# Key products of the first batch of null and masked attention inside the normalisation; null weights loaded during the routed experts

## The chip, the cores and the metric

One core of a Trainium2 chip runs the whole kernel. The metric is device time in microseconds (us); the median of three runs before the change is 2725.27 us (2724.52 to 2727.11).

## The reference

Eight residual layers on x of shape (8 batches, 256 positions, 256 features), all float32. Each adds a function of the normalised x to x. In order: a depooling layer, attention with registers, attention over a context, routed experts, null attention, a feed-forward layer with signs as weights, masked attention, and a last block with attention over positions and experts.

```python
x = x + _L1_ffn_ref(_layernorm(x, axis=-1), L1_ffn_router_w, L1_ffn_w1, L1_ffn_w2)
x = x + _L2_xattn_ref(_layernorm(x, axis=-1), ctx_2048, L2_xattn_Wq, L2_xattn_Wkv, L2_xattn_null_kv, ...)
x = x + _L2_ffn_ref(_layernorm(x, axis=-1), L2_ffn_k0, L2_ffn_k1, L2_ffn_k2, ...)
x = x + _L3_xattn_ref(ctx_2048, _layernorm(x, axis=-1), mask_BxS2_fk1, mask_BxS2_fk1, L3_xattn_W_src, ...)
```

Null attention has 16 heads of 64: queries from the normalised x, keys and values from the context (8, 256, 512), and one learned key and value more. Masked attention has 8 heads of 32; its keys, too, come from the context alone. So the keys of both need nothing of the layer's own normalisation.

## The kernel before

Activations are stored feature by position: `X` and `XN` are [128 partitions, 2, 2048 positions]. A layer is a row of blocks; at the end of a block all engines meet at a barrier. Inside a block each engine has a queue of its own, written out in order, and waits on semaphores of the others.

**Normalisation** (`layer_norm_phase`, L187). The 2048 positions are four groups (0 to 3) of 512. TensorE (L227 to L267) first makes the mean sums of all four groups, each in its own PSUM bank (4 to 7), then spreads means 0 and 1 over the partitions; then, per group: `variances` (sum of squares), `spread_mean` two groups ahead, `spread_inverse`. `chunk_sums` (L232) and `spread` (L238) are the helpers under whose lines its matmuls stand. ScalarE (ACT) loads its table for the square root if it isn't there (L288), copies the mean sums (L291), squares (L275) and takes roots (L279). VectorE (DVE) centres (L309), inverts (L316) and scales (L330). SyncE (SP) issues the layer's loads here (`prefetch`), and GpSimd (POOL) does `prepare`; the phase ends when all are through.

**Attention stream** (`attention_stream`, L554). One block after the normalisation. Before the first scores come the uses in `first`: in null attention a product of null values with output weights (L790), then the twelve products `front` of batch 0: query (L1649) and key (L1660) products in turn, four of each, and four value products (L1672). In masked attention: query (L1918), key (L1931) and value (L1945) product. Each goes into a PSUM bank (0 to 3 in turn) and is taken from there by VectorE or ScalarE. From then on the products of the next batch are interleaved with scores, exponentials and values by a fixed plan. The context of each batch is loaded in this block by SyncE, two batches ahead at most.

**Loads.** Null attention's weights are loaded in its normalisation (L1625 to L1631). Masked attention's are loaded in its own normalisation, first the mask row (L1895), which GpSimd turns into `drop` and `mrows` (L1906, L1907), then the weights (L1898).

**Routed experts** (L1374): four groups of eight experts; SyncE waits in that block for the experts' weights and has nothing else to do.

Of the kernel before, what the change touches and what calls it, by code (L numbers as in the profile page):

```python
# [82 lines left out]
def build(nc, A, out):  # L83
    top = ExitStack()
    with top:
# [43 lines left out]
        if STAGES >= 3:  # L129
            context_attention_layer(g)  # L130
            end_layer()
        if STAGES >= 4:
            routed_ffn_layer(g)
            end_layer()
        if STAGES >= 5:
            null_attention_layer(g)
            end_layer()
# [49 lines left out]
def layer_norm_phase(g, tag, src=None, dst=None, gain=None, shift=None, resid=None, rms_gain=None, eps=None,  # L187
                     prefetch=None, prepare=None, by_position=False, loaded=None, aside=None):
# [16 lines left out]
    def part(t, gi):  # L205
        return t[:, :, gi * GT:(gi + 1) * GT]

    with nc.Block() as block:
# [19 lines left out]
        def _(pe):  # L228
            def chunk_sums(bank, c0, of):
                for k in range(KD):  # L230
                    for c in range(4):
                        mm = pe.matmul(bank[32 * c:32 * c + 32, c0:c0 + P], mean[:, 0:32], of[:, k, c * P:(c + 1) * P],  # L232
                                       start=(k == 0), stop=(k == KD - 1))
                return mm
# [35 lines left out]
        def _(act):  # L270
# [6 lines left out]
            def root(gi):  # L277
                act.wait_ge(var_ready, gi + 1)
                act.activation(g.ln_std[:, gi % 2], g.bank[4 + gi][:, P:2 * P], ACT.Sqrt, bias=eps[:]).then_inc(rooted, 1)  # L279
# [9 lines left out]
            for gi in range(NG):  # L289
                act.wait_ge(mean_ready, gi + 1)  # L290
                act.activation(g.ln_mean[:, gi], g.bank[4 + gi][:, 0:P], ACT.Copy).then_inc(mean_copied, 1)  # L291
# [14 lines left out]
        def _(v):  # L306
# [32 lines left out]
            for gi in range(NG):  # L339
# [3 lines left out]
                scale(gi)  # L343
            v.wait_ge(scaled, NG)
# [209 lines left out]
def attention_stream(g, ctx, tag, heads, dh, groups, keys, front, front_at, q_of, k_of, v_of, slot_of, project, finish,  # L554
                     wl, n_weights, mask=None, own_keys=False, load=None, n_loads=0, load_after=None, null=None, reg=None):
# [35 lines left out]
    ld = [g.sem(f"{tag}_loaded{j}") for j in range(2)] if n_loads else None  # L591
# [36 lines left out]
    first += [("front", 0, k) for k in range(len(front))]  # L628
    slots = []
# [37 lines left out]
    def shared_bank(use):  # L667
        n = ready_at[use] - 1
        return g.bank[n % 4] if n < len(first) else M

    with nc.Block() as block:
        @block.sync
        def _(sp):
            if n_loads:
                for b in range(B):
# [24 lines left out]
        def _(pe):  # L700
# [60 lines left out]
            def shared(use):  # L761
                bank = shared_bank(use)
                before = ready_at[use] - 1 - (4 if ready_at[use] <= len(first) else 1)
                if before >= (0 if ready_at[use] <= len(first) else len(first)):
# [55 lines left out]
            for use in first:  # L820
# [30 lines left out]
        def _(act):  # L851
# [38 lines left out]
            for use in first:  # L890
# [33 lines left out]
        def _(v):  # L924
# [78 lines left out]
            for use in first:  # L1003
# [370 lines left out]
def routed_ffn_layer(g):  # L1374
# [18 lines left out]
    with ExitStack() as ctx:  # L1393
# [208 lines left out]
def null_attention_layer(g):  # L1602
    nc, A = g.nc, g.A
# [3 lines left out]
    with ExitStack() as outer:  # L1607
        gain = g.sb("na_gain", [P, KD], F32, outer)
        shift = g.sb("na_shift", [P, KD], F32, outer)
        with ExitStack() as ctx:  # L1610
            sb = lambda n, s, dt=F32: g.sb("na_" + n, s, dt, ctx)
            Wq = sb("Wq", [P, KD, INNER])
            Wkv = sb("Wkv", [P, KC, 2 * INNER])
            Wo = sb("Wo", [P, IC, D])
            cxT = sb("cxT", [P, 2, KC, N])
# [3 lines left out]
            nv = sb("nv", [P, IC, H])  # L1619
            nk = sb("nk", [P, IC])  # L1620
            wl, nkl, placed = g.sem("na_weights"), g.sem("na_null_loaded"), g.sem("na_null_placed")

            def prefetch(sp):
                for half in range(2):
                    sp.dma_start(nk[half * DH:(half + 1) * DH, :], A["L2_null_key"]).then_inc(nkl, 16)  # L1625
                sp.dma_start(Wq[:], feature_rows(A["L2_xattn_Wq"])).then_inc(wl, 16)
                sp.dma_start(Wkv[:], feature_rows(A["L2_xattn_Wkv"])).then_inc(wl, 16)
                sp.dma_start(Wo[:], feature_rows(A["L2_xattn_Wout"])).then_inc(wl, 16)
                sp.dma_start(nv[:].rearrange("p k h -> p (k h)"), A["L2_null_values"]).then_inc(wl, 16)
                sp.dma_start(gain[:], A["L2_xattn_ln_scale_col"]).then_inc(wl, 16)  # L1630
                sp.dma_start(shift[:], A["L2_xattn_ln_bias_col"]).then_inc(wl, 16)  # L1631
# [7 lines left out]
            layer_norm_phase(g, "n2x", prefetch=prefetch, prepare=prepare)  # L1639
# [5 lines left out]
            for m0 in range(0, IC, 2):  # L1645
# [11 lines left out]
                def k_product(pe, bank, b, m0=m0):  # L1657
                    for m in range(2):
# [25 lines left out]
            def finish(v, bank, b):  # L1684
# [9 lines left out]
                             null={"values": nv, "out": Wo})  # L1694
# [176 lines left out]
def masked_attention_layer(g):  # L1871
    nc, A = g.nc, g.A
    H, DH = 8, 32
    with ExitStack() as ctx:
# [16 lines left out]
        wl, ml, st = g.sem("ma_weights"), g.sem("mk_loaded"), g.sem("mk_step")  # L1891

        def prefetch(sp):
# [3 lines left out]
            for t, name in ((Ws, "L3_xattn_W_src"), (Wt, "L3_xattn_W_tgt"), (Wo, "L3_xattn_W_out")):  # L1897
# [4 lines left out]
            sp.dma_start(bv[:], A["L3_xattn_b_src"][D:2 * D].unsqueeze(0)).then_inc(wl, 16)  # L1902
# [7 lines left out]
        layer_norm_phase(g, "n3x", prefetch=prefetch, prepare=prepare)  # L1910
# [512 lines left out]
```

## Time and profile before

| | us |
|---|---|
| median of 3 runs | 2725.27 |
| the profiled execution | 2728.62 |
| its span in the trace | 2726.7 |
| TensorE busy | 2361.6 (87%) |
| VectorE busy | 1294.5 (47%) |
| ScalarE busy | 995.9 (37%) |
| GpSimd busy | 128.2 (5%) |

The span is the time from the first to the last instruction in the profile. Times in the rows are counted from its start. A float32 product of the program stands in the trace as two matmuls. PEclk is TensorE's granted clock, where 1.00 is 2.4 GHz and 0.50 is 1.2 GHz.

### The profile page before, as it was taken

Reading aid. Unit: us, or ns where it says so; the run is one execution under the profiler, and the core shown is the slowest. Engines: PE = TensorE matmul, PEld = TensorE weight load, DVE = VectorE, ACT = ScalarE, POOL = GpSimd, SP = SyncE. Lnnn points to the kernel's source line nnn. Section 1 sums busy time; section 2 is a strip of 40 time slices with the busy share of each in tenths; the row PEclk is TensorE's granted clock in tenths of the full one; section 3 lists DMA queues with packets and bytes.
Section 4 is the critical chain, followed back from the end, with each engine's and each line's share of the span. In section 5 each row is a group of like instructions: output and inputs, shape, how many; then the busy total and the mean of one; then the engine's idle time right before and its main releaser. Section 6 shows DMA issues by size and latency. Waiting matters only on the chain. (4 is left out here: it accounts for less than half of the span.)

```text
span 2726.7 us, 38491 instructions
## 1 busy us (share of the span) xinstructions
PE 2361.6 (87%) x15045; PEld 1680.3 (62%) x15045; DVE 1294.5 (47%) x2609; ACT 995.9 (37%) x2834; POOL 128.2 (5%) x206
## 2 busy tenths in 40 slices
PE   6778887999988999989999999969988897874984
PEld 4455555666655666666666666547876675654773
DVE  6456665777764334333455445654443443231003
ACT  3245564777762111112333333433223442231122
POOL 0000000000000000000000000030010000002003
PEclk8979999999998999999999999999999999796996
DMA  3000001000002000020000000000011000021332
GB/s 113 16 1 1 1 1 40 13 25 13 24 1 93 1 0 1 1 109 8 9 9 9 8 9 1 1 28 0 1 43 40 20 5 16 1 72 61 124 113 66
DMA packets 52534, 74.81 MB, mean 27 GB/s; under 512 B 8050, under 2 KB 41348, under 8 KB 51204
## 3 DMA queue, kind: packets, MB, share of 16 engines
q1 hardware_dynamic: 50820, 68.14, 7.4%
q0 software_dynamic: 1536, 4.20, 0.5%
q8 instruction: 123, 2.02, 0.3%
q14 instruction: 55, 0.45, 0.1%
HBM read 63.94 MB, written 8.39 MB: 27 GB/s over the span
## 5 line engine op out<-in xcount | busy, mean ns | idle before, releaser
L862 ACT ACTIVATE ca_prob<-bank,ca_nmax 128x512 f32<-128x512 f32 x256 | 174.0, 690 | 92.9 <-DVE ca_nmax L929 92.9
L929 DVE TENSOR_REDUCE ca_nmax<-bank 128x1 f32<-128x512 f32 x256 | 164.0, 682 | 56.2 <-PE bank L720 56.1
L862 ACT ACTIVATE na_prob<-bank,na_nmax 128x257 f32<-128x257 f32 x256 | 118.0, 474 | 191.0 <-DVE na_nmax L929 191.0
L1458 PE MATMUL bank<-XN,rf_W 128*128 128x512 f32 x384 | 172.9, 601 | 0.0
L1469 PE MATMUL bank<-rf_W,rf_h 128*128 128x256 f32 x768 | 170.8, 379 | 0.0
L1469 PEld LDWEIGHTS bank<-rf_W,rf_h 128*128 128x128 f32 x768 | 145.9, 190 | 33.1 <-issue 14.8
L734 PEld LDWEIGHTS bank<-cst,ca_prob 128*128 128x128 f32 x1024 | 112.3, 142 | 73.6 <-issue 63.2
L862 ACT ACTIVATE ra_prob<-bank,ra_nmax 128x256 f32<-128x256 f32 x256 | 118.2, 482 | 104.1 <-DVE ra_nmax L929 104.1
L1513 ACT ACTIVATE rf_r<-bank 128x512 f32<-128x512 f32 x96 | 57.4, 598 | 256.3 <-PE bank L1458 256.3
L734 PE MATMUL bank<-cst,ca_prob 128*128 128x128 f32 x1024 | 140.5, 279 | 6.6 <-DVE ca_pT L935 5.9
L929 DVE TENSOR_REDUCE na_nmax<-bank 128x1 f32<-128x257 f32 x256 | 90.8, 417 | 91.5 <-PE bank L720 91.5
L1660 PE MATMUL bank<-na_cxT,na_Wkv 128*128 128x256 f32 x512 | 117.8, 383 | 5.5 <-DVE na_q L1654 5.5
L1458 PEld LDWEIGHTS bank<-XN,rf_W 128*128 128x128 f32 x384 | 73.2, 193 | 79.8 <-issue 78.7
L1566 DVE TENSOR_TENSOR rf_h<-rf_r 128x512 f32<-128x512 f32 x96 | 66.1, 692 | 113.9 <-ACT rf_r L1513 113.9
L1778 PE MATMUL bank<-sf_h,sf_W 128*128 128x512 f32 x512 | 120.1, 395 | 0.0
L1672 PE MATMUL bank<-na_Wkv,na_cxT 128*128 128x512 f32 x256 | 115.4, 595 | 0.0
L1660 PEld LDWEIGHTS bank<-na_cxT,na_Wkv 128*128 128x128 f32 x512 | 95.0, 190 | 25.9 <-DVE na_q L1654 11.8
L1778 PEld LDWEIGHTS bank<-sf_h,sf_W 128*128 128x128 f32 x512 | 95.9, 187 | 23.5
L720 PE MATMUL bank<-ca_k,ca_qz 32*128 32x512 f32 x512 | 73.7, 642 | 26.0 <-ACT ca_prob L862 25.1
L935 DVE COPY ca_pT<-bank 128x512 f32<-128x512 f32 x128 | 87.4, 683 | 17.4 <-PE bank L734 17.2
L238 PE MATMUL bank<-ln_rstd,cst 128*128 128x128 f32 x352 | 51.8, 291 | 49.8 <-DVE ln_rstd L316 49.8
L929 DVE TENSOR_REDUCE ra_nmax<-bank 128x2 f32<-128x512 f32 x128 | 82.0, 681 | 22.4 <-PE bank L720 22.4
(395 smaller groups left out, 4423.8 us busy)
## 6 DMA issues: line engine op xcount, KB each, us to landing
xl_w<-in_L_ffn_w SPq DMA_DIRECT2D x16, 1024.0 KB
dp_cx<-in_ctx_tok SPq DMA_DIRECT2D x4, 1024.0 KB, 14.1
ca_v<-in_ctx_values SPq DMA_DIRECT2D x8, 512.0 KB, 4.6
rf_W<-in_L_ffn_w SPq DMA_DIRECT2D x8, 512.0 KB, 8.6
na_Wkv<-in_L_xattn_Wkv SPq DMA_DIRECT2D x1, 4096.0 KB
na_cxT<-in_ctx SPq DMA_DIRECT2D x8, 512.0 KB, 3.4
ma_cxT<-in_ctx SPq DMA_DIRECT2D x8, 512.0 KB, 3.3
X<-in_x SPq DMA_DIRECT2D x1, 2048.0 KB, 7.9
```

The lines of the kernel that those rows point to most:

```text
L720: mm = pe.matmul(S[u][:, hh * keys:(hh + 1) * keys], q_of(hs[hh], i, b), k_of(hs[hh], i, b), start=(mask is None), stop=(hh == per - 1), s ...
L734: mm = pe.transpose(TB[f % 2][:, j * P:(j + 1) * P], prob[:, n % 2, u, c0:c0 + P], ident)
L862: e = act.activation(prob[:, n % 2, u, hh * keys:(hh + 1) * keys], S[u][:, hh * keys:(hh + 1) * keys], ACT.Exp, bias=nmax[:, n % 2, u, hh: ...
L929: v.tensor_reduce(nmax[:, n % 2, u], S[u][:, 0:W].rearrange("p (h k) -> p h k", h=per), AX.X, ALU.max, negate=True).then_inc(maxed, 1)
L935: v.tensor_copy(o, TB[f % 2][:].rearrange("p (j q) -> p j q", j=4)).then_inc(copied_v, 1)
L1458: mm = pe.matmul(g.bank[n % 3][:], W1[:, k, c * P:(c + 1) * P], g.XN[:, k, gi * GT:(gi + 1) * GT], start=(k == 0), stop=(k == KD - 1))
L1469: mm = pe.matmul(output(i, t), h[:, n % 8, t * P:(t + 1) * P], W2[:, n % CH], start=(n == own[0]), stop=(n == own[-1]), skip_group_check=True)
L1513: act.activation(r[:, n % 3], g.bank[n % 3][:], ACT.Relu).then_inc(relu, 1)
L1566: v.tensor_tensor(h[:, n % 8], r[:, n % 3], r[:, n % 3], ALU.mult).then_inc(squared, 1)
L1660: mm = pe.matmul(bank[:, m * N:(m + 1) * N], Wkv[:, k, (m0 + m) * P:(m0 + m + 1) * P], cxT[:, b % 2, k], start=(k == 0), stop=(k == KC - 1))
L1672: mm = pe.matmul(bank[:], cxT[:, b % 2, k, t * P:(t + 1) * P], Wkv[:, k, INNER + half * 512:INNER + (half + 1) * 512], start=(k == 0), sto ...
L1778: mm = pe.matmul(g.bank[m % 4][:], W1[:, k, m * P:(m + 1) * P], h[:, k, s], start=(k == 0 and s == 0), stop=(k == C1 - 1 and s == 1))
```

## The change

The normalisation gets `fill`, an object with halves of key products to issue between its own matmuls and with copies to make behind its own copies. To free banks 6 and 7 for them, mean sums and variances of four groups share banks 4 and 5. Null attention issues key products `front[1]` and `front[3]` of batch 0 at places 0 to 3; place 0 is before `variances(0)`, place n behind `variances(n - 1)`. Masked attention issues its one key product at places 2 and 3. The stream leaves these out of `first`. Null's weights and the context of its batch 0 are allocated before the routed experts and loaded by SyncE in that block. Masked attention loads the context of batch 0 with its weights, in a new order.

```diff
 def layer_norm_phase(...)
+    def mean_at(gi):
+        return slice(gi // 2 * P, (gi // 2 + 1) * P)
+    def var_at(gi):
+        return slice(2 * P + gi // 2 * P, 2 * P + (gi // 2 + 1) * P)
...
             def variances(gi):
                 pe.wait_ge(squared, gi + 1)
-                chunk_sums(g.bank[4 + gi], P, g.ln_sq[:, gi % 2]).then_inc(var_ready, 1)
+                if gi >= 2:
+                    pe.wait_ge(rooted, gi - 1)
+                chunk_sums(g.bank[4 + gi % 2], var_at(gi), g.ln_sq[:, gi % 2]).then_inc(var_ready, 1)
...
             for gi in range(NG):
-                chunk_sums(g.bank[4 + gi], 0, part(src, gi)).then_inc(mean_ready, 1)
+                if gi >= 2:
+                    pe.wait_ge(mean_copied, gi - 1)
+                chunk_sums(g.bank[4 + gi % 2], mean_at(gi), part(src, gi)).then_inc(mean_ready, 1)
             spread_mean(0)
             spread_mean(1)
+            if fill is not None:
+                fill.multiply(pe, 0)
             for gi in range(NG):
                 variances(gi)
+                if fill is not None:
+                    fill.multiply(pe, gi + 1)
                 if gi + 2 < NG:
                     spread_mean(gi + 2)
                 spread_inverse(gi)
...
                 root(gi)
+                if fill is not None:
+                    fill.take(act, "a", gi + 1)
...
                 scale(gi)
+                if fill is not None:
+                    fill.take(v, "v", gi + 1)
 def attention_stream(...)
+    early_uses = [("front", 0, k) for k, _ in early]
+    first = early_uses + [use for use in first if use not in early_uses]
...
+        if n < len(early):
+            return g.bank[6 + n % 2]
+        return g.bank[(n - len(early)) % 4] if n < len(first) else M
...
+        def multiply(pe, place):
+            for n, (k, places) in enumerate(early):
+                for half in range(2):
+                    if places[half] == place:
+                        if half == 0:
+                            pe.wait_ge(wl, 16 * n_weights)
+                            if n_loads:
+                                pe.wait_ge(ld[0], 16 * n_loads)
+                            if n >= 2:
+                                wait_freed(pe, early_uses[n - 2])
+                        mm = front[k][1](pe, shared_bank(early_uses[n]), 0, half)
+                        if half == 1:
+                            mm.then_inc(ready, 1)
+        def take(engine, who, place):
+            for n, (k, places) in enumerate(early):
+                if places[1] == place and freer(early_uses[n]) == who:
+                    engine.wait_ge(ready, n + 1)
+                    front[k][2](engine, shared_bank(early_uses[n]), 0).then_inc(freed_v if who == "v" else freed_a, 1)
+    if norm is not None:
+        norm(Early)
...
-                for b in range(B):
+                for b in range(0 if norm is None else 1, B):
...
 def routed_ffn_layer(g, next_weights):
...
                 for e in range(E):
                     sp.wait_ge(weights[e], 32)
+                next_weights.load(sp)
...
+    def load(self, sp):     # class NullWeights
+        for half in range(2):
+            sp.dma_start(self.nk[half * self.DH:(half + 1) * self.DH, :], A["L2_null_key"]).then_inc(self.null_loaded, 16)
+        sp.dma_start(self.Wkv[:], feature_rows(A["L2_xattn_Wkv"])).then_inc(self.loaded, 16)
+        sp.dma_start(self.cxT[:, 0], feature_rows(A["ctx"][:, 0:N])).then_inc(self.context_loaded[0], 16)
+        sp.dma_start(self.Wq[:], feature_rows(A["L2_xattn_Wq"])).then_inc(self.loaded, 16)
...
 null attention:
+                             null={"values": nv, "out": Wo}, norm=norm, early=[(1, (0, 1)), (3, (2, 3))],
+                             ld=w.context_loaded)
 masked attention:
         def prefetch(sp):
+            sp.dma_start(Ws[:], feature_rows(A["L3_xattn_W_src"])).then_inc(wl, 16)
+            sp.dma_start(bv[:], A["L3_xattn_b_src"][D:2 * D].unsqueeze(0)).then_inc(wl, 16)
+            sp.dma_start(cxT[:, 0], feature_rows(A["ctx"][:, 0:N])).then_inc(context_loaded[0], 16)
             m1 = A["mask_BxS2_fk1"].rearrange("b n -> (b n)")
             sp.dma_start(mrow[:], m1.unsqueeze(0).to_broadcast([P, T])).then_inc(ml, 16)
...
         def k_take(v, bank, b):
+            if b == 0:
+                v.wait_ge(ml, 32)
...
+                         norm=norm, early=[(1, (2, 3))], ld=context_loaded)
```

## Rows read from the trace of the kernel before

**Rows 1.** The page: busy time by engine, and a kind of DMA issue.
```profile
PE 2361.6 (87%) x15045; PEld 1680.3 (62%) x15045; DVE 1294.5 (47%) x2609; ACT 995.9 (37%) x2834; POOL 128.2 (5%) x206
...
ma_cxT<-in_ctx SPq DMA_DIRECT2D x8, 512.0 KB, 3.3
```

**Rows 2.** Timeline, null's normalisation: start us, length us, instruction, [idle before and releaser].
```profile
1202.06 0.64 PE L232 MATMUL bank<-ln_sq,cst 128*32 128x128 f32 x16 [1.51 <-ACT ln_sq L275]
...
1202.64 1.16 PE L238 MATMUL bank<-ln_mean,cst 128*128 128x128 f32 x8
...
1204.30 1.16 DVE L309 TENSOR_TENSOR ln_cent<-X,bank 128x1024 f32<-128x1024 f32 x1
...
1205.64 1.22 DVE L330 TENSOR_TENSOR XN<-ln_cent,bank 128x1024 f32<-128x1024 f32 x1 [0.17 <-PE bank L238]
...
1209.05 1.22 DVE L330 TENSOR_TENSOR XN<-ln_cent,bank 128x1024 f32<-128x1024 f32 x1 [0.17 <-PE bank L238]
...
1211.26 1.16 PE L238 MATMUL bank<-ln_rstd,cst 128*128 128x128 f32 x8 [1.68 <-DVE ln_rstd L316]
...
1215.79 1.22 DVE L330 TENSOR_TENSOR XN<-ln_cent,bank 128x1024 f32<-128x1024 f32 x1 [1.25 <-PE bank L238]
```

**Rows 3.** Timeline, head of null's attention stream.
```profile
1217.55 3.61 PE L790 MATMUL bank<-na_Wo,na_nv 128*16 128x256 f32 x16 [1.80 <-PEq L208]
...
1222.93 3.62 PE L1660 MATMUL bank<-na_cxT,na_Wkv 128*128 128x256 f32 x16
...
1226.38 1.89 PE L1649 MATMUL bank<-XN,na_Wq 128*128 128x256 f32 x8
1226.64 0.60 ACT L1665 ACTIVATE na_k<-bank 128x512 f32<-128x512 f32 x1 [13.21 <-PE bank L1660]
```

**Rows 4.** Timeline, masked normalisation and head of its stream.
```profile
2031.32 7.11 POOL L1906 TENSOR_SCALAR ma_drop<-ma_mrow 128x2048 bf16<-128x2048 f32 x1 [185.18 <-DMA ma_mcol<-in_mask_col]
...
2035.08 0.65 PE L232 MATMUL bank<-ln_sq,cst 128*32 128x128 f32 x16
...
2038.50 5.38 POOL L1907 TENSOR_SCALAR ma_mrows<-ma_mrow 128x2048 f32<-128x2048 f32 x1
...
2045.35 1.22 DVE L330 TENSOR_TENSOR XN<-ln_cent,bank 128x1024 f32<-128x1024 f32 x1 [1.25 <-PE bank L238]
...
2047.09 1.97 PE L1918 MATMUL bank<-XN,ma_Wt 128*128 128x256 f32 x8 [1.78 <-PEq L208]
...
2052.29 5.15 PE L1931 MATMUL bank<-ma_cxT,ma_Ws 128*128 128x256 f32 x16 [3.24 <-DMA ma_cxT<-in_ctx]
...
2057.37 0.69 PE L1943 MATMUL bank<-ma_bv,cst 1*128 1x256 f32 x2
2057.48 0.88 DVE L1937 SCALAR_TENSOR_TENSOR ma_k<-bank,ma_bs,ma_mrow 128x256 f32<-128x256 f32 x2 [7.44 <-PE bank L1931]
...
2063.57 0.40 PE L716 MATMUL bank<-ma_drop,onesb 1*128 1x512 bf16 x4 [1.04 <-issue]
```

**Rows 5.** Windows, masked: stretch, length, busy time by engine, PEclk, DMA share, GB/s.
```profile
2033.00:2034.00 1.00, 0.36 (x5) 0.17 (x3) 1.00 (x2) 0.00 (x0) 1.00 (x1) 1.00 1.06 385
...
2036.00:2037.00 1.00, 0.81 (x8) 0.62 (x6) 1.00 (x2) 0.36 (x2) 1.00 (x1) 1.00 0.07 18
...
2052.00:2053.00 1.00, 0.71 (x2) 0.62 (x3) 0.00 (x0) 0.00 (x0) 0.00 (x0) 0.50 0.07 25
```

**Rows 6.** Timeline, mean sums and first copies in three other normalisations.
```profile
438.78 1.95 PE L232 MATMUL bank<-X,cst 128*32 128x128 f32 x64 [2.56 <-PEq L102]
...
440.15 0.92 ACT L291 ACTIVATE ln_mean<-bank 128x128 f32<-128x128 f32 x4
...
822.40 3.11 PE L232 MATMUL bank<-X,cst 128*32 128x128 f32 x64 [2.01 <-PEq L102]
...
2262.34 2.65 PE L232 MATMUL bank<-X,cst 128*32 128x128 f32 x64 [2.00 <-PEq L102]
```

**Rows 7.** Windows, first routed expert products behind the normalisation at 822.
```profile
846.00:850.00 4.00, 4.00 (x14) 3.16 (x15) 0.00 (x0) 0.39 (x2) 0.00 (x0) 0.50 0.00 0
```

More of the change, by code:

```diff
@@ L554, in attention_stream @@
 def attention_stream(g, ctx, tag, heads, dh, groups, keys, front, front_at, q_of, k_of, v_of, slot_of, project, finish,
-                     wl, n_weights, mask=None, own_keys=False, load=None, n_loads=0, load_after=None, null=None, reg=None):
+                     wl, n_weights, mask=None, own_keys=False, load=None, n_loads=0, load_after=None, null=None, reg=None,
+                     norm=None, early=(), ld=None):
     nc = g.nc
@@ L590, in attention_stream @@
                                       "widened", "scaled"))
-    ld = [g.sem(f"{tag}_loaded{j}") for j in range(2)] if n_loads else None
+    if ld is None and n_loads:
+        ld = [g.sem(f"{tag}_loaded{j}") for j in range(2)]
     S = [g.bank[u] for u in range(4)]
@@ L763, in shared @@
                 before = ready_at[use] - 1 - (4 if ready_at[use] <= len(first) else 1)
-                if before >= (0 if ready_at[use] <= len(first) else len(first)):
+                if before >= (len(early) if ready_at[use] <= len(first) else len(first)):
                     wait_freed(pe, order[before])
@@ L818, in shared @@
                 mm.then_inc(ready, 1)
-            for use in first:
+            for use in first[len(early):]:
                 shared(use)
@@ L888, in shared @@
                 e.then_inc(freed_a, 1)
-            for use in first:
+            for use in first[len(early):]:
                 shared(use)
@@ L1001, in shared @@
                     v.wait_ge(reg_inverted, use[1] + 1)
-            for use in first:
+            for use in first[len(early):]:
                 shared(use)
@@ L1606, in null_attention_layer, with __init__ @@
     IC = INNER // P
[L1607 to L1610, printed above, removed]
+    def __init__(self, g, outer, ctx):
+        sb = lambda n, s: g.sb("na_" + n, s, F32, ctx)
+        self.g = g
+        self.gain = g.sb("na_gain", [P, KD], F32, outer)
+        self.shift = g.sb("na_shift", [P, KD], F32, outer)
+        self.Wq = sb("Wq", [P, KD, self.INNER])
+        self.Wkv = sb("Wkv", [P, KC, 2 * self.INNER])
+        self.Wo = sb("Wo", [P, self.IC, D])
+        self.nv = sb("nv", [P, self.IC, self.H])
+        self.nk = sb("nk", [P, self.IC])
+        self.cxT = sb("cxT", [P, 2, KC, N])
+        self.loaded, self.null_loaded = (g.nc.alloc_semaphore(name="na_" + n) for n in ("weights", "null_loaded"))
+        self.context_loaded = [g.nc.alloc_semaphore(name=f"na_loaded{j}") for j in range(2)]
@@ L1611, in null_attention_layer @@
+def null_attention_layer(g, w, outer, ctx):
+    nc, A = g.nc, g.A
+    H, DH, INNER, IC = w.H, w.DH, w.INNER, w.IC
+    gain, shift, Wq, Wkv, Wo, nv, nk, cxT, wl, nkl = (w.gain, w.shift, w.Wq, w.Wkv, w.Wo, w.nv, w.nk, w.cxT, w.loaded,
+                                                      w.null_loaded)
+    with outer:
+        with ctx:
             sb = lambda n, s, dt=F32: g.sb("na_" + n, s, dt, ctx)
[L1612 to L1613 removed]
@@ L1618, in null_attention_layer @@
             vv = sb("v", [P, 2, 2, INNER])
[L1619 to L1631, printed above, removed]
+            placed = g.sem("na_null_placed")
             def prepare(po):
@@ L1655, in q_take, with k_product @@
                                              None, ALU.mult)
-                def k_product(pe, bank, b, m0=m0):
-                    for m in range(2):
+                def k_product(pe, bank, b, half=None, m0=m0):
+                    for m in range(2) if half is None else (half,):
                         for k in range(KC):
@@ L1926, in q_take, with k_product @@
             return o
-        def k_product(pe, bank, b):
-            for m in range(KD):
+        def k_product(pe, bank, b, half=None):
+            for m in range(KD) if half is None else (half,):
                 for k in range(KC):
```

48 lines of the change are left out of this document (29 added, 19 removed).

## The prediction, made before the changed kernel was run

> **What bounds the kernel now.** I read the page's first two parts, then the timelines of the two stretches that the change rewrites, then the start of every other normalisation, and last the granted clock. TensorE is busy in 87% of the span and DVE in 47% [rows 1], so work taken off TensorE in a stretch that it bounds is time. The chain of waits on the page covers only the last 25 us, so each stretch is judged from its timeline.
>
> Each normalisation runs four groups in turn (0 to 3): TensorE sums squares, TensorE spreads the next mean and the inverse root, DVE inverts, centres, scales. In null's the scalings of groups 0 and 1 start 3.41 us apart (1205.64, 1209.05), and DVE fills that with a reciprocal, a centring of 1.16 and a scaling of 1.22. TensorE is not full: it stands idle 1.51 us before the first sum of squares and 1.68 us before the third spread of the inverse [rows 2]. After the barrier the picture turns round: from 1217.55 TensorE runs without a gap, with the null product (3.6 us), then query and key products in turn; the first key product begins at 1222.93 and the query product behind it at 1226.38, 3.45 us later, as in the pairs that follow [rows 3]. That stretch is bound by TensorE.
>
> Masked attention starts otherwise. TensorE does the query product at 2047.09, waits 3.24 us for batch 0's context, and does the key product in 5.15 us, not 3.6, since in the pause its clock went from 2.4 to 1.2 GHz (granted 0.50 in the slice from 2052) [rows 4, 5]. The value product follows at 2057.37 and the first scores at 2063.57.
>
> **Null attention, the stream.** Two key products leave the head of the stream: 2 x 3.45 = **6.9 us** less of unbroken TensorE work. The takers are no limit there: ACT needs 0.60 us for a key product, below the 1.73 us of the shortest product, and waits 13.21 us for its first [rows 3]. I take the full 6.9. Bounds: 0 (something else ends the head last, such as DVE's copies of the values) to 7.2 (two rows of 3.62).
>
> **Null attention, the normalisation.** The four halves cost 1.72 us each. Before sum 0 the pause is 1.51, so the first half costs 0.2. The second stands between the sum of squares 0 and the spread of mean 2, which DVE wants: that spread moves from 1202.64 to 1204.58, centring 2 from 1204.30 to 1205.76, and the scaling of group 0 from 1205.64 to 1206.93 (+1.3) [rows 2]. The third does the same to mean 3: sum of squares 1 at 1206.64, the half to 1208.94, the spread of mean 3, centring at 1210.13, scaling 1 at 1211.30 where it was 1209.05 (+2.25). The fourth falls into the pause of 1.68 us and costs nothing more by itself; square, root and reciprocal of group 2, now queued behind the late centring, bring the scalings 2 and 3 to +2.4. ACT's two copies of 0.60 stand in its idle time. The normalisation ends **2.4 us** later. Bounds: 1.3 (only the first displaced spread counts) to 5.2 (three halves outside the pause).
>
> The loads themselves move from SP's queue in the normalisation to that in the routed experts, behind that stage's own weights, which are down by its first items; nine DMAs run beside some 340 us of expert products. Before, nobody waited on them either: TensorE started 0.54 us after the last scaling of null's normalisation, and 0.52 after the masked one [rows 2, 3, 4]. So 0. Null's scalings beside such traffic (1205.64) and after it (1215.79) both take 1.22 us [rows 2]; a stretch of the last digit in them, 1%, over the 20 us that the loads last would be 0.2 us, the bound on either side. SP's own waits there are met some 300 us before the barrier.
>
> **Masked attention, the stream.** The key product and the wait for the context both go: the scores stood 16.48 us behind the start of the query product [rows 4]. Without them: query product 1.9, then from the first value product to the scores 6.2 (2057.37 to 2063.57), sum 8.1. Gain **8.4 us**, if the clock stays up, which it did until the pause. Bounds: 3.2 (the wait alone) to 8.4.
>
> **Masked attention, the normalisation.** Here the weights are not loaded ahead: the first half waits, behind sum of squares 1, for all seven loads. Before, the DMA engines were done with them at about 2036.3: 385 GB/s in the slice from 2033, 18 in that from 2036 [rows 5]. The context adds 512 KB ahead of them [rows 1]; at 385 GB/s that is 1.4 us, so about 2037.7. TensorE reaches the half at 2035.08 + 0.58 = 2035.66: a new wait of **2.0 us** (bounds 0 to 3). Behind it in TensorE's queue are the spread of mean 3 and of the inverse 1, which DVE waits for. With the half's 1.72 that spread starts at 2039.4 for 2035.66; DVE's own work had covered 0.6 of that, as in null's rounds (scaling 0 there waits 0.17, the centring ahead of it stands 0.5 behind its spread), so scaling 1 comes 3.1 later, 2.0 of it the wait. The second half falls in the pause. Then DVE takes the key product itself, two operations in 0.88 us [rows 4], between scaling 2 and reciprocal 3, on the chain that ends the phase: +0.9, and the rest of the shift through ACT's late root makes **4.2 us** in all. Bounds: 2.1 (no wait) to 5.2 (3 us of wait).
>
> GpSimd: the mask row now queues behind the context and a weight of twice its size, 1.57 MB; it came at 2031.32, and at 385 GB/s comes 4.1 us later, at 2035.4. Its 7.11 + 5.38 us [rows 4] end at 2047.9. The phase ends at 2046.57 + 4.2 = 2050.8 by DVE, so GpSimd has 2.9 us to spare. Were DVE not late it would end the phase at 2047.9, 1.3 us later than before; so that is the floor of this term if the wait is shorter.
>
> **All normalisations: two banks in place of four.** The mean sums of groups 2 and 3 now wait for ACT's copies of groups 0 and 1. ACT must first load its table and touch it: its first copy ends 1.63 us after TensorE's start (440.15 + 0.26 - 438.78) [rows 6]. TensorE at 2.4 GHz would begin sum 2 after 0.98 (64 matmuls in 1.95): a new pause of 0.70 us with the 0.05 of a signal, and everything of that phase comes later by it. This holds for context's normalisation and for the two at 1790.9 and 2437.9 which show the same 1.95 and 0.92: 3 x 0.70 = 2.1. At 2262.34 the sums take 2.65 and the clock falls among them; sum 2 would start at 2263.3, and now at 2264.0: 0.7. At 822.40, where they take 3.11, sum 2 would start at 823.8 and now at 824.1: 0.3. In the other six the sums run at 1.2 GHz from the start or no table is loaded, and the copy is there in time. Sum **3.2 us**; bounds 0 (the copies' timing hides it) to 11 x 0.7 = 7.7. The waits on the variance side are met long before.
>
> **The sum.** -6.9 + 2.4 - 8.4 + 4.2 + 3.2 = **-5.5 us**. The profiled execution took 2728.62 us, 1.9 beyond its span and 3.3 above the median of the runs; nothing in these terms scales with that, so they are taken off the median: 2725.27 - 5.5 = **2719.8 us**.
>
> **Rivals.** (A) is the sum above, with its likeliest terms: 2717.5 to 2722.
> (B) The fillings cost less: the mean sums don't pause, or the weights are there. Without the masked wait the phase ends at 2048.7 by DVE, 2.1 late and not 4.2: 2717.7. Without the 3.2 as well: 2714.5. For it: in the last slice of the loads only 18 GB/s moved, small transfers whose order is not seen. Against: TensorE has to wait for a count that includes the last of them.
> (C) The clock. After null's and the masked normalisation TensorE's clock was up (the query product's 8 matmuls of 256 columns in 1.97 us [rows 4]), but after the one at 822 it was at 0.50 for four us and more of expert products [rows 7]. The same phase with the same work ended in both ways. One such fall more (masked, where the normalisation gets a 2 us wait and a longer thin tail) costs half of its length. The row shows four us of it; I take ten, since the slices on either side of the row are slow in part, and so 5 us: 2724.8. The present one going away gives 2715.
> The Trainium skill ("TensorE: Matmul & The Clock Gate", Part 1) says that the throttled state is the default and activity releases it, and that the monitor runs free of the kernel's start. Rows 4 and 5 agree with the first half: idle from 2049, at 0.50 by 2052 [rows 4, 5]. By this rule a stall inside a thin phase is what makes (C); it also lets the filled null phase hold its clock better, and does not say which; it changes no term of the sum.
> (D) Slower: the new pauses behind the mean sums, each on top of the 2 to 3 us of idle at the barrier ahead, drop the clock in the four normalisations that have them and in the masked one. Priced as in (C), 5 us each; it decides from the third such fall: +15 - 5.5 gives 2734.8. Two leave 2729.8, still within 0.2%. Against it: 0.7 us is small beside the 1.5 us pauses that these phases have already with the clock up.
> That the products are not early at all is excluded: the order of the queues is written out.
>
> **How the numbers follow.** A measurement of this kernel can tell about 0.2%, 5.45 us, from no change; the forecast of -5.5 stands on that bound. (A) 0.42, half on either side; (B) 0.25, faster; (C) 0.20, within; (D) 0.08, slower; 0.05 for a better clock or an unseen cost. Faster 0.49, within 0.2% 0.42, slower 0.09. The range holds (A), (B) and most of (C), with room for one clock episode on either side: 2712 to 2728.
>
> **What would show it.** In null: key products at four places of the normalisation, its last scaling 2.4 us later against the phase's first sum, the stream's first scores 6.9 us earlier against its null product. In masked: a TensorE wait ahead of the first half that a DMA of the weights ends, 2 us; scaling 3 4.2 us later against the phase's start; no wait for the context, value products right behind the query product at clock 1.00; GpSimd done before DVE. In context's normalisation a TensorE idle of 0.7 us released by ACT's copy. Wrong it would be by a TensorE clock of 0.50 in a stretch where it is 1.00 now, by GpSimd ending the masked phase, or by a stream head that did not shorten by the product's time.

## The result and the profile after

The changed kernel takes 2736.91 us (median of 22 runs, 2724.11 to 2747.91), the kernel before 2726.07 (22 runs beside it, 2714.58 to 2732.61). The ratio is 1.0038, 95% interval 1.0024 to 1.0053: it is slower, where the prediction said 2719.8 and gave "slower" 0.09. Single runs of the changed kernel fall into two groups, eleven up to 2735.2 and eleven from 2738.6 on; the profiled execution, 2731.23 us, is of the first.

The page after shows nothing of it at first sight: TensorE is busy for 3.6 us more, and the line of its clock reads almost alike.

```profile
span 2729.4 us, 38507 instructions
PE 2365.2 (87%) x15045; PEld 1679.9 (62%) x15045; DVE 1294.9 (47%) x2609; ACT 996.1 (36%) x2834; POOL 128.3 (5%) x206
```

A table of stages tells more. A stage is taken here from ACT's first use of its square root (L288, L307 after) in one normalisation to that in the next. The stretch ahead of the first row (87.4 us before and after) and the one behind the last (33.2 before, 32.5 after) are left out. In y3 that use stands behind the copies, so its borders lie up to 4 us later. Times are us.

```
stage             before  again(z3)  after  x0     y1     y2     y3     x3     y4     z1
registers          352.7   349.7     354.8  354.9  355.0  349.7  351.4  352.6  351.2  351.5
context            383.6   387.5     389.6  389.6  388.5  385.5  385.1  383.6  383.7  385.5
routed experts     372.6   368.4     373.2  373.3  370.8  372.4  370.1  372.4  372.4  368.2
null               596.0   598.3     592.8  592.8  596.1  594.4  592.7  595.9  594.3  594.3
null, second norm.  23.9    23.9      26.0   26.0   26.2   23.7   25.2   23.7   23.7   23.7
signs              210.1   210.0     210.9  210.9  210.9  210.7  209.0  210.2  210.8  210.5
masked             237.4   237.4     240.0  240.1  234.4  240.5  245.0  233.9  235.3  236.3
positions          175.6   175.6     163.2  163.2  178.8  174.0  179.4  162.5  168.9  173.9
experts            254.4   254.7     259.1  255.0  255.7  254.3  252.9  255.2  254.2  254.5
```

(The labels are those of the experiments below.) Against the first trace of the kernel before, the changed kernel wins 3.2 us in null and loses 2.1 with registers, 6.0 in context, 2.1 and 0.8 around null's second normalisation and 2.6 in masked. Two traces of the kernel before differ by 3 to 4 us in registers, context and routed experts, so one pair of columns says little there. All fourteen traces together say more. The five with two banks and the early table (after, x0, y1, x1, x2) have registers at 354.5 to 355.0, context at 388.5 to 389.6 and null's second normalisation at 26.0 to 26.2; the nine others have 349.7 to 352.7, 383.6 to 387.5 and 23.7 to 25.3. In the profiled execution positions gives 12.4 back, in attention code that the change doesn't touch (of that stage it touches the normalisation). Had it stood at 175.6 there as well, this execution would have taken 2743.6, which is where the second group of runs lies; that is inferred, no execution of that group was profiled. TensorE's clock goes with the stage's time: over the whole of it the mean is 0.89 in the kernel before and 0.98 after. A window in it shows the same; the stage begins 11 us later after than before, so the three windows don't hold quite the same work.

Windows of 2360 to 2400, before, after and x1; columns as in [rows 5].

```profile
2360.00:2400.00 40.00, 34.61 (x185) 25.10 (x184) 11.29 (x29) 9.68 (x39) 1.23 (x2) 0.84 0.00 1
```

```profile
2360.00:2400.00 40.00, 33.64 (x207) 25.05 (x208) 13.09 (x33) 13.50 (x56) 1.23 (x2) 1.00 0.00 1
```

```profile
2360.00:2400.00 40.00, 34.92 (x174) 24.89 (x172) 9.99 (x26) 10.03 (x40) 0.61 (x1) 0.79 0.00 0
```

**Null.** The timeline after answers to [rows 2, 3]. The half at 1211.61 pushes the spread of mean 2 to 1213.44; the last scaling ends 2.4 us later against the phase's first sum, as forecast. Then the null product, 3.61 us before, takes 4.90: the clock has fallen at the end of the phase. The first scores come 33.4 us behind that product's start and not 39.1: a gain of 5.6, not 6.9. In all eight traces with null's early products this product takes 4.9 to 6.6 us; of the six without them, five have 3.61.

```profile
1213.44 1.05 PE L249 MATMUL bank<-ln_mean,cst 128*128 128x128 f32 x8
...
1226.95 1.22 DVE L351 TENSOR_TENSOR XN<-ln_cent,bank 128x1024 f32<-128x1024 f32 x1 [1.25 <-PE bank L249]
...
1228.72 4.90 PE L847 MATMUL bank<-na_Wo,na_nv 128*16 128x256 f32 x16 [1.80 <-PEq L219]
```

**Masked.** The timeline answers to [rows 4]. The first half waits 3.29 us for the last of seven loads and then runs at 1.2 GHz (3.42 us; the second half, at 2.4 GHz, 1.99). The phase takes 27.5 us from its first sum, 7.1 more than before. The context wait is gone, but query and value products run at 1.2 GHz again, and the scores come 12.15 us behind the query product where I had 8.1. GpSimd, started by the mask at 2045.12, is done at 2057.7, ahead of DVE.

```profile
2034.63 2.11 PE L243 MATMUL bank<-X,cst 128*32 128x128 f32 x64 [2.57 <-PEq L102]
...
2045.12 7.11 POOL L1988 TENSOR_SCALAR ma_drop<-ma_mrow 128x2048 bf16<-128x2048 f32 x1 [190.69 <-DMA ma_mcol<-in_mask_col]
...
2047.63 3.42 PE L2014 MATMUL bank<-ma_cxT,ma_Ws 128*128 128x256 f32 x8 [3.29 <-DMA ma_bo<-in_L_xattn_b_out_col]
...
2060.90 1.22 DVE L351 TENSOR_TENSOR XN<-ln_cent,bank 128x1024 f32<-128x1024 f32 x1 [1.25 <-PE bank L249]
...
2062.64 3.75 PE L2001 MATMUL bank<-XN,ma_Wt 128*128 128x256 f32 x8 [1.78 <-PEq L219]
...
2074.79 0.40 PE L773 MATMUL bank<-ma_drop,onesb 1*128 1x512 bf16 x4 [1.03 <-issue]
```

**Context**, where no product was moved, loses most against the first trace before. The timeline answers to [rows 6]: the two first mean sums take 1.08 us, then TensorE is idle for 0.60 us until ACT has copied the first, as forecast. But the other two and the spreads then run at 1.2 GHz (1.71 and 3.02 us, the spreads 2.05 before), and once more the first 16 matmuls of the next block: 6.64 us, 3.69 before.

```profile
440.91 1.08 PE L243 MATMUL bank<-X,cst 128*32 128x128 f32 x32 [2.56 <-PEq L102]
...
442.58 1.71 PE L243 MATMUL bank<-X,cst 128*32 128x128 f32 x32 [0.60 <-ACT ln_mean L310]
444.23 3.02 PE L249 MATMUL bank<-ln_mean,cst 128*128 128x128 f32 x16
...
464.20 6.64 PE L1343 MATMUL bank<-XN,ca_Wqkv 128*128 128x256 f32 x16 [1.81 <-PEq L219]
```

Windows of the same two places:

```profile
442.00:446.00 4.00, 3.42 (x40) 3.02 (x41) 0.00 (x0) 1.24 (x6) 0.71 (x1) 0.61 0.83 260
...
464.00:468.00 4.00, 3.80 (x9) 3.11 (x10) 0.00 (x0) 0.00 (x0) 0.00 (x0) 0.50 0.64 180
```

### The profile page after: what moved, and what is told of

Its sections match the earlier page's. It is cut to its first block and busy times, and to the rows that moved or that the text cites. A ratio compares the mean times of both kernels' runs of the same rounds, so it can differ in the third digit from the quotient of the medians.

```text
span 2729.4 us, 38507 instructions
## 1 busy us (share of the span) xinstructions
PE 2365.2 (87%) x15045; PEld 1679.9 (62%) x15045; DVE 1294.9 (47%) x2609; ACT 996.1 (36%) x2834; POOL 128.3 (5%) x206
## 3 DMA queue, kind: packets, MB, share of 16 engines
q8 instruction: 123, 2.02, 0.3%
## 5 line engine op out<-in xcount | busy, mean ns | idle before, releaser
L992 DVE COPY ca_pT<-bank 128x512 f32<-128x512 f32 x128 | 87.4, 683 | 17.2 <-PE bank L791 17.2
L1637 DVE SCALAR_TENSOR_TENSOR rf_acc<-bank,rf_comb,rf_acc 128x256 f32<-128x256 f32 x112 | 49.0, 479 | 90.9 <-PE bank L1527 90.9
## 6 DMA issues: line engine op xcount, KB each, us to landing
na_Wkv<-in_L_xattn_Wkv SPq DMA_DIRECT2D x1, 4096.0 KB, 13.2
```

Of the source, the lines that this page charges most:

```text
L992: v.tensor_copy(o, TB[f % 2][:].rearrange("p (j q) -> p j q", j=4)).then_inc(copied_v, 1)
```

## The experiments

Three sets (x, y, z) of four kernels; those of a set share a chip and the runs of the kernel before (medians 2724.29, 2725.25, 2725.44). Each had 10 to 12 runs.

### x0_after_again: the changed kernel once more

> The changed kernel once more, as a yardstick for the three beside it and for a second trace. All theories: about 10 us slower than before. If its single runs fall again into two clusters (about 2727 and 2742), then the trace with the lower mean granted clock (0.948 to 0.950 against 0.954) shows in which stage the second cluster loses its time.

Measured: 2727.16 us (2720.05 to 2745.82), ratio 1.0028 (1.0004 to 1.0051). Nine runs to 2733, three from 2742 on. The trace is of the first group and repeats the one above stage by stage but for experts (column x0); so no trace shows the second group. The kernel is slower again, though its interval begins just above 1 and its median lies 9.8 us below the first; its losses in registers and context are no accident of one execution.

### x1_masked_undone

```diff
-        def norm(early):
-            layer_norm_phase(g, "n3x", prefetch=prefetch, prepare=prepare, fill=early)
+        layer_norm_phase(g, "n3x", prefetch=prefetch, prepare=prepare)
...
-                         norm=norm, early=[(1, (2, 3))], ld=context_loaded)
+                         )
```

The masked layer's loads, their order and the place of its first context go back too.

> The changed kernel with the masked layer as it was (no early key product, context loaded in the stream, old order of loads). Theory M (the masked half's wait for all seven loads, 3.3 us in the trace and not 2.0, plus the clock that falls in that wait and again at the end of the phase): 3 to 8 us faster than the changed kernel, so +3 to +7 us against before. Theory B (the waits of the mean sums in all eleven normalisations): no difference to the changed kernel, +10.

Measured: 2730.87 (2724.09 to 2735.85), ratio 1.0023 (1.0008 to 1.0038). Against x0 the median is 3.7 higher and the mean 0.4 higher (2730.8, 2730.4): no difference. Its masked stage is 6 us shorter than x0's (234.1), but positions stands at 176.3 where x0 had 163.2. Theory M is not needed for the loss and alone does not undo it. The undone layer shows something else. Its key product waits 1.37 us for the context here, not 3.24, keeps its clock, and the scores stand 13.18 us behind the query product, not 16.48:

```profile
2057.61 3.72 PE L2010 MATMUL bank<-ma_cxT,ma_Ws 128*128 128x256 f32 x16 [1.37 <-DMA ma_cxT<-in_ctx]
```

Of the eight traces with the masked layer undone or never changed, five are like this (x1, x2, x3, y1, y4: waits of 1.27 to 1.43) and three like [rows 4] (before, z3, z4: 3.18 to 3.24). Which one comes is not explained by any run.

### x2_loads_and_banks

Both early products undone, as above for masked, and for null:

```diff
-                layer_norm_phase(g, "n2x", prepare=prepare, fill=early)
+                layer_norm_phase(g, "n2x", prepare=prepare)
...
-                             null={"values": nv, "out": Wo}, norm=norm, early=[(1, (0, 1)), (3, (2, 3))],
+                             null={"values": nv, "out": Wo}, norm=norm,
```

> No early product anywhere: what is left of the change is two banks in place of four for the sums of all normalisations, and null's weights and first context loaded during the routed experts. Theory B: +3 by the pauses alone, up to +10 with clock falls behind them. Theory M: +3 and no more. Rival L (loads during the routed experts cost): as here, and in the next kernel too.

Measured: 2735.55 (2729.36 to 2745.01), ratio 1.0046 (1.0030 to 1.0062). With nothing left but banks and loads it is as slow as the whole change. Theory B or rival L.

### x3_loads_only

As x2, with four banks (`g.bank[4 + gi]`, columns 0 and 128) and without the two waits.

> Only null's weights and first context loaded during the routed experts; four banks, no early product, the masked layer as before. Theories M and B: no difference to before (within 2 us). Rival L: slower, +3 or more.

Measured: 2717.43 (2710.07 to 2723.83), ratio 0.9972 (0.9959 to 0.9986): faster than before, which neither theory had. Rival L falls. Between x2 and x3 lie only the banks and their waits: 18.1 us by the medians, more than the whole change costs; of the difference between their traces, 13.6 us stand in positions. The trace says where x3 gains against before, not why: positions 162.5 and masked 233.9; null and routed experts stand as before.

### y1_two_banks_pure

The kernel before, with

```diff
             for gi in range(NG):
-                chunk_sums(g.bank[4 + gi], 0, part(src, gi)).then_inc(mean_ready, 1)
+                if gi >= 2:
+                    pe.wait_ge(mean_copied, gi - 1)
+                chunk_sums(g.bank[4 + gi % 2], mean_at(gi), part(src, gi)).then_inc(mean_ready, 1)
```

and the same for the variances.

> The kernel before with one edit: sums of four groups in two banks, with the two waits for ACT's copies. Theory B (the pause of 0.6 to 0.7 us behind the second mean sum starts falls of TensorE's clock in context's, null-end's and expert normalisations): +8 to +14 us against before, with context's stage 5 to 6 us longer. Rival (the loads in the routed experts and the two banks cost only together): within 3 us of before.

Measured: 2733.57 (2726.85 to 2743.99), ratio 1.0036 (1.0021 to 1.0052), the size of the whole change. Theory B holds, with context 4.9 longer than in the first trace before, though only 1.0 longer than in z3. Its timeline in context has the pause of 0.60, slow sums behind it, and the slow head of the next block:

```profile
440.55 1.08 PE L238 MATMUL bank<-X,cst 128*32 128x128 f32 x32 [2.56 <-PEq L102]
442.23 1.83 PE L238 MATMUL bank<-X,cst 128*32 128x128 f32 x32 [0.60 <-ACT ln_mean L301]
...
463.90 6.55 PE L1296 MATMUL bank<-XN,ca_Wqkv 128*128 128x256 f32 x16 [1.80 <-PEq L214]
```

The cleanest place is null's second normalisation. In all nine traces without the pause its 64 sums run through at 2.4 GHz (1.95 to 2.11 us); in all five with it the second 32 fall to 1.2 (1.93 to 1.94 where the first took 1.08). Before, and y1:

```profile
1790.92 1.95 PE L232 MATMUL bank<-XN,cst 128*32 128x128 f32 x64 [1.05 <-PEq L671]
```

```profile
1797.65 1.93 PE L238 MATMUL bank<-XN,cst 128*32 128x128 f32 x32 [0.60 <-ACT ln_mean L301]
```

### y2_four_banks_elsewhere

```diff
+    shared = fill is not None
...
-                if gi >= 2:
+                if shared and gi >= 2:
                     pe.wait_ge(mean_copied, gi - 1)
```

with bank and columns by `shared` too.

> The changed kernel, but the nine normalisations that get no early product keep four banks and no wait. Theory B: 8 to 12 us faster than the changed kernel, so -3 to +2 against before. Theory M (masked is the cost): no more than 3 us faster than the changed kernel.

Measured: 2728.34 (2720.82 to 2729.32), ratio 1.0012 (0.9999 to 1.0024): 8.6 us below the median first measured for the changed kernel, though not below x0's, and with +3.1 by the medians just outside the -3 to +2 expected. Registers and context stand at 349.7 and 385.5. The masked stage keeps its loss (240.5). Its first half waited 2.02 us this time:

```profile
2036.52 3.63 PE L2015 MATMUL bank<-ma_cxT,ma_Ws 128*128 128x256 f32 x8 [2.02 <-DMA ma_bo<-in_L_xattn_b_out_col]
```

### y3_table_later

The changed kernel, two banks everywhere, with ACT's table load moved:

```diff
-            act.activation(g.hold[:], eps[:], ACT.Sqrt).then_inc(table_set, 1)
             for gi in range(NG):
                 act.wait_ge(mean_ready, gi + 1)
                 act.activation(g.ln_mean[:, gi], ...).then_inc(mean_copied, 1)
+            act.activation(g.hold[:], eps[:], ACT.Sqrt).then_inc(table_set, 1)
             square(0)
```

> The changed kernel with two banks everywhere, but ACT loads its square root table behind its four copies of the mean sums and not ahead of them, so that the copies are in time and the pause goes. Theory B in the form that the pause is the cause: as good as four banks, 8 to 12 us faster than the changed kernel. Rival (two groups in one bank are slow for another reason, such as the matmul writes and the copies meeting in a bank): no gain.

Measured: 2723.50 (2715.69 to 2736.50), ratio 0.9996 (0.9979 to 1.0013): 13.4 below the changed kernel's first median, 3.7 below x0's. Its interval lies clear of the changed kernel's first (1.0024 to 1.0053) and overlaps x0's a little. It is no slower than y2, which has four banks elsewhere: two groups in a bank do no harm, the pause does. No TensorE wait for the copies is left in its trace. That execution is one of its slower ones (2730.15): masked stands at 245.0, where the clock fell in the wait for the loads (3.33) and stayed down longer than in the other traces, and positions at 179.4. In context the 64 sums run through and the block behind starts at 2.4 GHz:

```profile
436.64 2.11 PE L243 MATMUL bank<-X,cst 128*32 128x128 f32 x64 [2.56 <-PEq L102]
...
457.74 3.69 PE L1343 MATMUL bank<-XN,ca_Wqkv 128*128 128x256 f32 x16 [1.80 <-PEq L219]
```

### y4_null_only_four

As y2, with the masked layer undone as in x1.

> The part of the change that should pay by theories M and B together: null's early products and its loads ahead, four banks in the other ten normalisations, the masked layer as before. Loads only measured about -7, null's part was -3 by the traces: -7 to -11 us against before. If null's early products cost by the clock: worse than loads only, above -7.

Measured: 2718.60 (2715.89 to 2727.09), ratio 0.9984 (0.9970 to 0.9998), by the medians -6.7, by the ratio -4, where -7 to -11 was expected; 9.7 below y2, which differs by the masked part only. So in company of four banks theory M holds. Against x3 null's early products gave nothing: its null stage is 1.6 shorter, the whole not. In this trace the clock falls behind the filled phase, and the null product takes 6.55 us for 3.61:

```profile
1217.52 6.55 PE L848 MATMUL bank<-na_Wo,na_nv 128*16 128x256 f32 x16 [1.80 <-PEq L220]
```

### z1_masked_needs_only

```diff
-            sp.dma_start(Ws[:], feature_rows(A["L3_xattn_W_src"])).then_inc(wl, 16)
+            sp.dma_start(Ws[:], feature_rows(A["L3_xattn_W_src"])).then_inc(keys_loaded, 16)
+            sp.dma_start(bs[:], A["L3_xattn_b_src_col"]).then_inc(keys_loaded, 16)
...
-                            pe.wait_ge(wl, 16 * n_weights)
+                            pe.wait_ge(early_wl or wl, 16 * (early_n or n_weights))
```

> Four banks in the nine normalisations without early products (as in y2), and the masked half waits only for what it reads: the source weights, their bias and the context, issued first. Theory M: its wait of 3.3 us and the clock fall in it go, GpSimd (mask row behind 1.5 MB) becomes the end of the phase; masked stage 234 to 236 us where y2 had 240.5, and 3 to 6 us faster than y2. Rival (the masked stage loses by the place of the product, not by the wait): as y2, 2728.

Measured: 2720.12 (2714.93 to 2721.63), ratio 0.9979 (0.9969 to 0.9989), 8.2 below y2, of another set. The wait is gone, the masked stage is at 236.3, 4.2 below y2's. The traces' other 4.2 us stand in routed experts, which this edit doesn't touch. GpSimd ends the phase now, as forecast: its second pass ends at 2043.29, DVE's last scaling at 2042.45, and TensorE starts 0.49 behind GpSimd, at 1.2 GHz again.

```profile
2037.91 5.38 POOL L1991 TENSOR_SCALAR ma_mrows<-ma_mrow 128x2048 f32<-128x2048 f32 x1
...
2041.23 1.22 DVE L352 TENSOR_TENSOR XN<-ln_cent,bank 128x1024 f32<-128x1024 f32 x1 [1.25 <-PE bank L250]
...
2043.78 3.75 PE L2003 MATMUL bank<-XN,ma_Wt 128*128 128x256 f32 x8 [2.59 <-PEq L220]
```

### z2_masked_places_3_4

As z1, with `early=[(1, (3, 4))]`.

> As z1, with the masked halves one place later (behind the sums of squares 2 and 3), where TensorE has its pauses of 1.7 us. Theory M: nothing stands ahead of the spread of mean 3 any more, so the phase ends up to 1 us earlier than in z1, unless GpSimd ends it in both; then as z1.

Measured: 2720.30 (2717.66 to 2724.21), ratio 0.9982 (0.9969 to 0.9996), masked 236.3: as z1.

### z3_before_again: the kernel before once more

> The kernel before once more, as a yardstick of how far two samples of one kernel lie apart, and for a second trace of it. All theories: ratio 1.000, within 0.1%. In the trace: the masked context lands after 3.2 to 4.2 us as in six of the experiments, not 5.6, so the masked stage is 234 us and not 237.4; the position stage is at 163 or at 176.

Measured: 2725.36 (2717.66 to 2730.49), ratio 0.9993 (0.9980 to 1.0006). Two samples of one kernel may thus lie 0.07% apart, inside the interval. The masked part of the expectation missed: the context wait is 3.18 us, the key product 5.17, the stage 237.4 again, so the long wait of [rows 4] came in both traces of this kernel. Registers, context and routed experts move by 3 to 4 us between them. And context loses its clock here without any pause: the sums begin at 1.2 GHz (3.22 us, 1.95 in [rows 6]), and so does the head of the next block (6.28 us for 3.69).

```profile
435.81 3.22 PE L232 MATMUL bank<-X,cst 128*32 128x128 f32 x64 [2.56 <-PEq L102]
...
458.37 6.28 PE L1286 MATMUL bank<-XN,ca_Wqkv 128*128 128x256 f32 x16 [1.80 <-PEq L208]
...
2051.27 5.17 PE L1931 MATMUL bank<-ma_cxT,ma_Ws 128*128 128x256 f32 x16 [3.18 <-DMA ma_cxT<-in_ctx]
```

### z4_loads_and_table

x3's loads, and the late table of y3.

> Loads only (x3, about 7 us faster than before) with ACT's table loaded behind its copies of the mean sums in all normalisations. If the late table is a gain of its own (the first copy 0.9 us earlier where TensorE is at 2.4 GHz, nothing else late): 0 to 3 us faster than x3, 2714 to 2717. If it delays the first squares: slower than x3. No theory of the change hangs on it; it asks for the best version.

Measured: 2719.72 (2711.37 to 2727.41), ratio 0.9981 (0.9966 to 0.9996). No gain on x3 is seen (the intervals overlap widely), though it brings ACT's first copy 0.7 us forward (0.70 us behind the first sum, 1.37 in x3); the late table is seen to pay only where two banks make TensorE wait for the copies.

The best version measured is x3, loads alone: 0.9972 (0.9959 to 0.9986).

## Why the prediction was wrong

**The step that failed** is the term "all normalisations: two banks in place of four". It had the mechanism (sum 2 waits for a copy that the table load delays) and the length of the pause (0.70; the traces show 0.60). It priced the pause at its own length, 3.2 us in all, and put its effect on TensorE's clock into rival (D), with 0.08, on the ground that 0.7 us is small beside pauses of 1.5 us. Measured alone (y1) the term is worth 0.36% (0.21 to 0.52), 8 to 10 us. Removing the pause and keeping the two banks (y3) removes the loss, and the late table that does it gains nothing by itself (z4). In context the pause begins 1.1 us behind the barrier's 2.6 us of idle, and the five traces that have it show the clock down behind it and again at the head of the next block. The five traces hold 28 such pauses; behind 22 the next 32 matmuls ran at 1.2 GHz for most of their length. (D)'s threshold, three falls of 5 us, was nearly what came, in smaller pieces. From the median of the nine traces without the pause to that of the five with it: 4.3 in context, 3.5 with registers, 2.3 in null's second normalisation. The clock is the likely carrier, not a proven one: no run changed the clock alone, and z3 shows that context can lose it without a pause.

I also took normalisations whose sums run at 1.2 GHz as safe, by one trace. At 86 us before, the 64 matmuls of the sums took 3.40 us; after, the first 32 took 1.08, at 2.4 GHz, and the pause of 0.6 came there too. The other way round, the one at 2437.9 was counted and had no pause after (3.43 us for the 64). Which sums are slow is not a property of the place: z3, the kernel before once more, has 1.95 at 86.

**Masked, the normalisation: 4.2.** It came to 7.1. The wait was 3.29 for 2.0, and the half behind it held TensorE 3.26 us for 1.72, since the clock had fallen in the wait: 4.2 + 1.3 + 1.6. The half began 13.0 us behind the phase's first sum, in the changed kernel and in y2 alike. The working had 11.5 (2037.7 less 2026.17), because it took the end of the bulk traffic for the landing of the last load. After, the rate is down to 127 GB/s in the slice from 2045 and 15 in that from 2046, and TensorE is let go at 2047.63. In y2 the wait is only 2.02 because the mean sums ran at 1.2 GHz (3.35 us for 2.11) and TensorE came later, not the loads earlier; its phase is 7.3 us longer than before. The wait is confirmed as a cost by z1: without it DVE's last scaling ends 2.3 us later than before against the phase's start.

**Masked, the stream: 8.4.** Half of it came, 4.3. Most of the 8.4 was the context's wait of 3.24 us and the slow key product behind it. In the five traces of the old masked stream where the wait was 1.27 to 1.43, the scores stand at 13.1 to 13.2; measured from there the gain in the head is 1.0. The condition named, "if the clock stays up", failed in the changed kernel, y2 and z1 alike: query product 3.75 us for 1.97. Between its last two spreads TensorE now waits 2.38 us for DVE's key copy and reciprocal in y2 and z1, 1.60 before. The fall of the clock was rival (C).

**Null, the normalisation: 2.4** came to the digit, +2.4, with the spread of mean 2 at the computed place. **Null, the stream: 6.9** came to 5.6, and in y4 to 4.0: the clock fell behind the filled phase, though I had thought the filling would help it hold.

**Loads: 0, bounds 0.2.** Wrong in the good direction: x3 is 7 us below before. No load wait and no stage of null accounts for it; in its one trace the gain stands in positions (-13.1) and masked (-3.5). A small part is seen in every kernel with the loads moved: TensorE's idle ahead of the normalisations at 1195, 1816, 2026 and 2262 is 0.15 to 0.17 us shorter (2.03 to 1.87, 6.04 to 5.87, 2.72 to 2.57, 2.00 to 1.83), 0.65 in all. The five kernels with loads ahead, no pause in the nine other normalisations and no masked wait for weights (x3, y4, z1, z2, z4) all lie at 0.997 to 0.998. Whether the early loads have to do with positions' clock stays open: that stage took 175.6 to 178.8 us in the three traces without them and 162.5 to 179.4 in the eleven with them.

**GpSimd's 2.9 us to spare**: 4.4 in the changed kernel, whose phase ended late; and it did end the phase once the wait was gone (z1), as said.

**The sum.** In the stage table of the profiled execution: registers +2.1, context +6.0, null -3.2, second normalisation and signs +2.9, masked +2.6, routed experts and experts +5.3 (of which 4.7 in experts, 0.6 in x0), positions -12.4; and what is not in the table -0.6. The total, +2.7, hides that the changed parts lost 10 us, about what the medians say, because positions, whose attention lies outside the change, stood 12.4 us better. It did so in both traces of the changed kernel (163.2 and 163.2), as it stood at 175.6 in both of the kernel before.

The chance of 0.49 for faster came from a sum of terms of 3 to 8 us, each of them read from one execution, in a kernel in which two traces of the same program differ by 4 us in a single stage. The term for the banks was 3.2 in it, and the masked layer's two terms (-4.2 together) came to +2.8. The range of 2712 to 2728 allowed one clock episode; eleven normalisations were touched.

## What to carry to other kernels

A wait that is added to a helper is paid at every call of the helper. Before pricing it at its own length, look at what TensorE did in the microseconds around it: here a short pause on top of a barrier cost more than its own length, with the clock down behind it and at the head of the next block. And a wait that is to go is a gain of that size only against the kernel in which it was read: the context's wait stood at 3.2 us in three traces and at 1.3 to 1.4 in five, with the same masked layer. Make shared machinery (here the bank split) conditional on the case that needs it, and let an early product wait for its own operands only.

## What the runs showed of the hardware

- In the five traces with two banks and the early table, 28 pauses of 0.48 to 0.60 us stand between two runs of 32 matmuls. Behind 22 of them the second 32 took 1.64 to 1.94 us, at 1.2 GHz for most of it, where the first took 1.08 to 1.20; behind six they took 1.08. In context (2.56 us of idle, 1.08 of matmuls, 0.60 of pause) it fell in all five, and so did the clock at the head of the next block some 20 us later (6.51 to 6.71 us for 3.69).
- The pause is not the only way there. Of the nine traces without it, three have context's sums at 1.2 GHz from their start (z3 3.22 us, y2 3.34, z4 3.33), and z3 has the slow head as well (6.28).
- The positions stage, whose attention no kernel changed, took 162.5 to 179.4 us in fourteen traces, with a mean clock over the stage of 0.89 before and 0.98 after; the two traces of the kernel before gave 175.6 both.
- ACT's copies did not need the square root's table: with its load behind them (y3) the first copy in context began 0.70 us behind the first sum (1.37 before), and the first root stood 4.54 us behind the start of the spreads, as before.
- The last of ten loads of the masked layer, of 1 KB, let TensorE go 1.6 us behind the slice in which the bulk of 3.3 MB ended (2045 to 2046, let go at 2047.63).
